# Where VectorE adds the expert results of batches 4 to 7, and in which order SyncE issues the loads of the next batch

## The reference

```python
x = x + 0.5 * L0_ffn(layernorm(x))        # 8 experts, top 2, capacity 256
x = x + L0_attn(layernorm(x))             # 16 heads of 8, keys and values from a strided depthwise convolution (256 keys)
x = x + 0.5 * L0_ffn(layernorm(x))
x = x + 0.5 * L1_ffn(layernorm(x))        # causal attention with its own layer norm, then 16 experts, top 2
x = x + L1_attn(layernorm(x))             # causal attention, 16 heads
x = x + 0.5 * L1_ffn(layernorm(x))
```

## Time and profile before

| | us |
|---|---|
| median of 3 runs | 2228.93 (2227.15 to 2235.24) |
| the profiled execution, its own time | 2219.2 |
| its span | 2217.5 |
| PE busy | 1635.7 (74%) |
| DVE busy | 1380.3 (62%) |
| ACT busy | 979.6 (44%) |
| POOL busy | 1014.6 (46%) |
| max tiles on DVE (L657), 1408 | 787.6, mean 611 ns |

### The profile page before, as it was taken

One profiled execution on the slowest core, in us unless ns is written; L12 is line 12 of the kernel. 1 busy time (PEld: TensorE's weight loads), 2 busy tenths in 40 slices (PEclk: granted clock), 3 DMA queues, 4 the chain that ended last, 5 costly groups with the idle time before them and its releaser, 6 DMA issues. The chain is left out here.

```text
span 2217.5 us, 45287 instructions
## 1 busy us (share of the span) xinstructions
PE 1635.7 (74%) x16814; PEld 929.4 (42%) x16816; DVE 1380.3 (62%) x3344; ACT 979.6 (44%) x2064; POOL 1014.6 (46%) x1706
## 2 busy tenths in 40 slices
PE   4434778873637999982687359999999999836872
PEld 3321333332514656651333135555656556523331
DVE  8538667746188777757321497777777777474213
ACT  1112566651214766661222127667666767511220
POOL 1233365530523657430577334536556674305772
PEclk9975899985858999996898669999999999867996
DMA  6242222210432323300244322332323233002444
GB/s 199 65 126 74 57 70 72 76 38 27 139 86 60 103 79 84 103 22 24 62 102 87 104 84 75 92 85 75 103 71 92 79 89 98 22 24 58 95 86 129
DMA packets 226872, 178.20 MB, mean 80 GB/s; under 512 B 33447, under 2 KB 215599, under 8 KB 226272
## 3 DMA queue, kind: packets, MB, share of 16 engines
q1 hardware_dynamic: 211232, 154.74, 24.6%
q0 software_dynamic: 10240, 17.96, 4.0%
q10 hardware_dynamic: 5184, 2.63, 0.4%
HBM read 104.34 MB, written 72.35 MB: 80 GB/s over the span
## 5 line engine op out<-in xcount | busy, mean ns | idle before, releaser
L657 DVE TENSOR_REDUCE mx<-PS 128x2 f32<-128x512 f32 (+3 forms) x1408 | 787.6, 611 | 255.5 <-PE PS L358 171.3
L530 ACT ACTIVATE pt<-PS 128x512 f32<-128x512 f32 (+2 forms) x1408 | 667.1, 533 | 363.7 <-PE PS L358 263.4
L373 PE MATMUL PS<-ka,qa 48*128 48x256 bf16 (+3 forms) x2048 | 503.6, 308 | 86.7 <-DVE mx L657 80.1
L482 PE MATMUL PS<-qa,ka 51*128 51x512 bf16 (+3 forms) x1792 | 485.2, 319 | 31.3 <-DMA qa<-nm 31.2
L358 PE MATMUL PS<-mask_q,identh 64*128 64x128 bf16 (+1 forms) x3072 | 354.9, 206 | 0.0
L427 PE MATMUL PS<-pt,vs 128*32 128x512 f32 (+3 forms) x3584 | 348.6, 482 | 0.0
L358 PE MATMUL PS<-mask_k,identh 64*128 64x64 bf16 (+1 forms) x3072 | 343.3, 202 | 0.0
L1174 POOL DMA_INDIRECT pt<-xn_rows,idx x160 | 165.3, 1033 | 333.7 <-DVE idx L1109 286.1
L767 POOL CAST nm<-nm 16x128 bf16<-16x128 f32 x128 | 36.0, 281 | 593.3 <-ACT nm L562 581.2
L358 PEld LDWEIGHTS PS<-mask_k,identh 64*128 64x128 bf16 x3072 | 270.3, 95 | 54.1 <-issue 1.8
L358 PEld LDWEIGHTS PS<-mask_q,identh 64*128 64x128 bf16 x3072 | 275.3, 97 | 26.5 <-issue 6.8
(11 more groups left out here) (212 smaller groups left out, 2363.0 us busy)
## 6 DMA issues: line engine op xcount, KB each, us to landing
pt<-in_f_w SPq DMA_DIRECT2D x96, 256.0 KB, 3.2
q_parts<-parts SPq DMA_DIRECT2D x192, 128.0 KB, 2.4
qa<-q_parts SPq DMA_DIRECT2D x256, 96.0 KB, 2.4
k_parts<-parts SPq DMA_DIRECT2D x144, 128.0 KB, 2.4
ka<-k_parts SPq DMA_DIRECT2D x192, 96.0 KB, 2.4
xn_rows<-xn SPq DMA_DIRECT2D x32, 256.0 KB, 2.3
xn<-y_rows SPq DMA_DIRECT2D x32, 256.0 KB, 4.8
hid<-y_rows SPq DMA_DIRECT2D x32, 256.0 KB, 5.4
```

The costliest lines, as they stand in the source:

```text
L373: mm = pe.matmul(PS[:, bank, i * n:(i + 1) * n], k.qa[rows, b % 2, g, h // 2, qb * P:(qb + 1) * P], k.ka[rows, b % 2, g, h // 2, 0:n], sta ...
L482: mm = pe.matmul(PS[:, bank, i * n:(i + 1) * n], k.ka[rows, b % 2, g, h // 2, kb * P:(kb + 1) * P], k.qa[rows, b % 2, g, h // 2, q0:S], st ...
L530: nc.scalar.activation(k.pt[:, u % 2, at[c]:at[c] + len(heads) * n], PS[:, SC_BANK + c % RING, 0:len(heads) * n], ACT.Exp, scale=SCORE_SCA ...
L657: nc.vector.tensor_reduce(out, PS[:, MX_BANK + t % RING, 0:len(heads) * n] .rearrange("p (h n) -> p h n", n=n), AX.X, ALU.max).then_inc(s. ...
```

## The change

1. The additions and moments of batches 4 to 7 leave the start. Each batch's three steps (first result, second result, moments) become events of one unit, placed between its last max tiles: batches 4, 5, 6, 7 in units 1, 2, 5, 6, at positions 8, 10, 11 of the causal attentions and 5, 6, 7 of the first. The inverse roots of the four batches together follow max tile 0 of unit 7. Both are in `when` (`late0`, `late1`, `late2`, `late_root`).
2. `norm` on DVE writes `xa` before the base; a new semaphore `base_ready` tells POOL of the base. `add_bias` of batches 0 and 1 moves on POOL from the end of unit 0 to the start, behind the four copies of the first values.
3. SP's loads of the next batch are issued one in each of the groups 0 to 3, not two in group 0 and two in group 1.

```diff
+    LATE_ENTRY = {1: 4, 2: 5, 5: 6, 6: 7}
...
+                "late0": 8, "late1": 10, "late2": 11, "late_root": 0}
...
+                "late0": 5, "late1": 6, "late2": 7, "late_root": 0}
...
+        if u in LATE_ENTRY:
+            events += [(name, LATE_ENTRY[u]) for name in ("late0", "late1", "late2")]
+        if u == max(LATE_ENTRY) + 1:
+            events += [("late_root", 3)]
...
+            def entry(step, b):
+                if step < 2:
+                    combine(nc, k, dve, seg(b).src, b, step)
+                else:
+                    dve.wait_ge(*s.combined.at(2 * b + 2))
+                    chain.link(moments(nc, k, chain, seg(b).src, b))
+
+            def entry_deviations(group):
+                first, n = ENTRY_GROUPS[group]
+                deviations(nc, k, chain, columns(first, n), seg(0).twice).then_inc(s.st_ready.h, 1)
...
-                if twice:
-                    normalise(nc.vector, k, src, b, k.rstd, lambda t: here(dst, b)[:, t * P:(t + 1) * P])
                 normalise(nc.vector, k, src, b, k.rstd2 if twice else k.rstd,
                           lambda t: k.xa[:, t, :]).then_inc(s.xa_ready.h, 1)
+                if twice:
+                    normalise(nc.vector, k, src, b, k.rstd,
+                              lambda t: here(dst, b)[:, t * P:(t + 1) * P]).then_inc(s.base_ready.h, 1)
...
-            for t in range(NMX):
-                max_tile(0, t)
-            enter(3)
-            for t in range(NMX):
-                max_tile(1, t)
+            for u in range(2):
+                for t in range(NMX):
+                    max_tile(u, t)
...
+                    elif name in ("late0", "late1", "late2"):
+                        entry(int(name[-1]), n)
+                    elif name == "late_root":
+                        entry_deviations(n)
...
-                pool.wait_ge(*s.xa_ready.at(b + 1))
+                pool.wait_ge(*(s.base_ready if seg(b).twice and b < 2 else s.xa_ready).at(b + 1))
...
             for g in range(G):
                 spread(0, g)
+            add_bias(0)
+            add_bias(1)
             split(0, 1)
...
-                if u == 0:
-                    add_bias(0)
-                    add_bias(1)
...
-                if g < 2 and b + 1 < NB:
-                    load(b + 1, 2 * g)
-                    load(b + 1, 2 * g + 1)
+                if b + 1 < NB:
+                    load(b + 1, g)
```

More of the change, by code:

```diff
@@ L286, in attention @@
         when = {"value_p": 2, "max_T": 2, "o_out": 2, "nm": 2, "o_T": 5, "value0": 8, "x_T": 8, "k": 8, "ctx_T": 8,
-                "q": 11, "v": 11, "out": 11, "value1": 11, "moments": 4, "f_moments": 4, "f_T": 8, "f_l": 11}
+                "q": 11, "v": 11, "out": 11, "value1": 11, "moments": 4, "f_moments": 4, "f_T": 8, "f_l": 11,
+                "late0": 8, "late1": 10, "late2": 11, "late_root": 0}
         early, late = ((0,), (1,)), (2, 3)
@@ L292, in attention @@
         when = {"value_p": 2, "max_T": 2, "o_out": 2, "nm": 2, "o_T": 4, "x_T": 5, "k": 5, "ctx_T": 5, "value0": 6,
-                "q": 7, "v": 7, "out": 7, "moments": 3, "f_moments": 3, "f_T": 5, "f_l": 7}
+                "q": 7, "v": 7, "out": 7, "moments": 3, "f_moments": 3, "f_T": 5, "f_l": 7,
+                "late0": 5, "late1": 6, "late2": 7, "late_root": 0}
         early, late = ((0,),), (1,)
@@ L601, in enter @@
                 for b in range(first, first + n):
[L602 to L606, removed]
+                    for step in range(3):
+                        entry(step, b)
+                entry_deviations(group)
             def later_moments(b):
@@ L899, in attention @@
     counts = {
-        s.ln_step: k.entry_steps, s.pl_step: k.pool_steps, s.st_ready: len(ENTRY_GROUPS), s.mo_ready: NB - B, s.fm_ready: B - 1, s.combined: 2 * B, s.xn_stored: 16 * B,
+        s.ln_step: k.entry_steps, s.pl_step: k.pool_steps, s.st_ready: len(ENTRY_GROUPS), s.mo_ready: NB - B, s.fm_ready: B - 1,
+        s.base_ready: 2 * seg(0).twice, s.combined: 2 * B, s.xn_stored: 16 * B,
         s.xa_ready: NB, s.ob_added: NB, s.xT_full: NB, s.xT_free: NB, s.q_full: NB,
@@ L1240, in __init__ @@
         self.ln_step = new("ln_step")
-        self.pl_step = new("pl_step")
+        self.pl_step, self.base_ready = new("pl_step"), new("base_ready")
         self.st_ready, self.mo_ready, self.fm_ready = new("st_ready"), new("mo_ready"), new("fm_ready")
```

## The result

The changed kernel takes 2205.39 us (median of four runs, 2187.72 to 2207.27), the one before 2229.26 beside it; the ratio is 0.9861, 95% interval 0.9825 to 0.9897. Forecast were 2173, in 2150 to 2198: the sign was right, and 24 of 56 us came. The profiled execution took 2205.91 us (span 2204.2), against the 2163.7 of the sum.

The account below looks back on a forecast made before the run. PE was taken to bound both causal loops, and to wait in the first loop and at the starts. Terms 54 + 11 + 8 + 2 - 17 - 2.5 = 55.5 us gave 2163.7 profiled, 2173 as median; range 2150 to 2198.

Parts of the forecast that it names:

- The root in unit 7: Inverse-root chain on DVE, nearly all reaching PE: 3.9 us in the second attention, 1.6 in the third.
- The starts: Entry of batches 4 to 7 leaves each attention's start: first scores 15, 20.7 and 18.4 us sooner, 54 in all.
- The bias additions: POOL's two additions beside DVE's entry at each start: collisions cost 0.8 us each, 2.5 in all, between 0 and 5.
- the 2 us of clock at the causal starts: Second and third attention starts: PE no longer rests 20 us before its first unit, so a higher clock gives 2 us.
- Two signs that the prediction had named for being wrong: Waits for loads appearing, or the maxima of unit 0 later than 662 in the second start, would refute the forecast.
- The late additions and moments: Late entry overfills DVE's gaps: PE loses 1.1, 0.5, 2.4, 0.5 us in the second attention; 1.1, 0.5, 1.8, 0.5 in the third.
- One load a group: First attention, batches 1 to 6: put_max goes out 1.84 us sooner, 11 us in all; 0 in the causal loops.
- rival C: Loads moved inside the loops come late and PE waits for them: 2260 at 1 us each; chance 0.03.
- The clock in the first attention: First loop: shorter waits give back 8 of 19 us, ends 0 and 15; mean clock 0.94 or more.
- rival B: Remaining waits of some 2 us still pull the clock down: 8 us not won, 2181; chance inside the forecast's 0.70.
- Rival A: Late steps are paid again in full in the loops, DVE becoming the bound: 2212, half of it 2193; chance 0.12.

## Why the prediction was wrong

- **The root in unit 7** is one of the two steps that failed most. It was priced at the 3.9 us of a quiet DVE, and 1.6 in the third attention, with no clock behind it; for the first it lay within 3. The marks of units 8 and 9 say 10 to 11, 2 to 5 and about 2 to 6 over the profiles. Two things were missing. In the second attention POOL's split stands beside the chain, and three of its instructions of 16 columns took 1.0 to 1.2 us instead of 0.17. And a wait of PE in a loop that ran at 2.4 GHz was followed by some us at 1.2: behind 4.09 to 6.83 us each time, behind 1.51 in four profiles of six. The prediction had a clock term for waits that go, and none for the wait that it put in.
- **The starts** were read right in their mechanism and too large: 11.7, 14.1 and 14.4 us at unit 1 for 15, 20.7 and 18.4. In all, 40 us for 54, a miss about as large as the root's. Four things were left out or too small. The bias additions cost 2.0, 2.7 and 1.5 us, where I took 0.8 each from the 1.75 of one collision; the bound of 5 for all three, too, was passed (6.2). DVE's wait of 1.2 us for PE had been hidden by the entry in the second and third. Once put_max(0) is early, the loads queued behind it are the next thing late, 1.8, 2.0 and 0.7 us, which I had not looked for there. And the 2 us of clock at the causal starts did not come: more of their first unit ran at 1.2 GHz than before (0.62 and 0.55, in a second profile 0.74 and 0.76, for 0.84 and 0.86). Two signs that the prediction had named for being wrong were there: waits for loads (those of batch 0), and maxima of unit 0 later than 662 in the second start. put_max(0) ends its issue at 646.65 us, which is 663.1 at the same distance from the start of the attention before.
- **The late additions and moments** cost 3 to 4 us in the second attention and 4 to 6 in the third between the marks of units 1 and 8, for 4.5 and 3.9 forecast: right in the second, somewhat low in the third.
- **One load a group** was right in size: 11 us of waits forecast, 12.1 measured, and rival C did not occur, since no load that was moved made PE wait. The waits left are larger than forecast: the prediction counted seven, 22.2 us, and let 9 remain; there were 18 of 0.3 us or more, 29.7 us, and 15 to 18 remained.
- **The clock in the first attention** was right for the loads alone (8 forecast, 11.9 measured) and wrong for the change, where PEclk went from 0.89 to 0.91 and not to 0.94: here rival B held. Besides the waits for the maxima PE has others in this loop, which the prediction did not count and no part of the change touches: for DVE's `ctx`, 19 us before and 20 after, and the clock fell behind such a one too (changed kernel):

```profile
395.63 1.07 PE L398 MATMUL PS<-ident,xa 128*128 128x128 f32 x4 [1.80 <-DVE ctx L686]
396.64 0.61 PE L489 MATMUL PS<-qa,ka 51*128 51x512 bf16 x1
```

  The rule that the prediction cites from the Trainium skill (TensorE: Matmul & The Clock Gate, section "HAM oscillation — how this bites in real kernels"), by which a wait for a DMA in each turn of a loop throttles PE again in each turn, agrees in kind: the clock fell in each of the eight batches of the changed kernel. It does not tell why the kernel with the loads alone, with as many waits left (17.6 us for the maxima, 20 for `ctx`), ran at 0.95 and this one at 0.91. Which of the moved steps holds it down was not found: with the root off DVE it was 0.91 as well.
- **Rival A** named the loss but not its way: of 40 us won by unit 1, 27 had been paid back by unit 9 (35 without the 7.7 that the loads give by then), yet DVE was not the bound, busy 234 of 300 us in the window shown; the root's chain and the clock behind it made about 20 of them.
- **The ends** were in no step. They differ by up to 10 us between executions of one kernel, and the profile of before, 9.7 us below its median, had drawn two short ones. I counted that difference in but did not ask where it came from; it would have shown the wait of 6.5 to 7.3 us in each, which was worth more than the whole change.

Put together: 22.5 - 0.5 + 5.6 = 27.6 us up to the last marks, near what the medians show (24 and 28). The ends take 14.7 of them back in the first profile, which leaves 12.9, and the two spans differ by 13.3: the ends decide which of the profiles looks better.

## What to carry to other kernels

Price a chain of small dependent instructions by what the other engine does in its new place, not by its quiet length, and count a new wait of PE in a loop at its upper clock at more than its length: here 4.09 us cost 8.0, 6.83 cost 10 to 11, and 1.51 cost 2.1 or 4 to 5, as the clock held or fell. When a start becomes earlier, read the queue behind the step that was waited for: what stood in its shadow is late next. If executions of one kernel differ, find the stretch in which they do; here it held the largest gain.

## What the runs showed of the hardware that was not expected

Even instructions of 128 x 16 elements on VectorE took 1.01 to 1.23 us instead of 0.17 beside GpSimd's split. Two of them ended within 0.03 us of a tensor operation of GpSimd of 1.17 us, the third with its copy and cast before; not all that ran beside the split were so long. That fits the rule of the Trainium skill (SBUF — State Buffer, section "SBUF: two separate sides") that the two lock each other out for a whole instruction, and shows what it costs a short one. The same 186 matmuls took 20.49 or 29.97 us in two executions of one kernel, at a mean granted clock of 0.75 and 0.50; with the wait ahead of them removed it was 0.87 to 0.91 over the ends of two kernels. And a wait of PE of 1.51 us, the same to 0.01 us in six profiles, was followed by the lower clock in four of them and not in two.
